# A transformer layer on one core: where the decay is multiplied in, how row maxima are taken and carried, and the order of the work

## The chip, the cores and the metric

The kernel runs on one core of one Trainium2 chip. The metric is the device time of one execution, in microseconds (us). A core has five engines that run their own instruction streams in order and wait for each other on semaphores: TensorE (PE, matrix products), VectorE (DVE), ScalarE (ACT), GpSimd (POOL) and SyncE (SP), which here only issues DMAs.

## The reference

The layer is a decayed quadratic attention plus a mixture of experts on the same normalised input. x is (4, 1024, 128). Cut to what the change touches:

```
qkvg = x @ w_attn                       # 16 query heads, 8 key/value heads, head size 64
q, k = rope(q), rope(k)
log_G = cumsum(log_sigmoid(6.906768 + gate), axis=time)
s = q . k / 8
logits = 2 * log|s| + log_G[t] - log_G[s]      # causal
a = exp(logits - max(logits))                  # so a is s*s*decay, over its row maximum
y = (a @ v) / (sum(a) + 1e-6)
y = (y - mean(y)) / sqrt(var(y) + 1e-9) * ln_w
out = x + y @ w_proj + experts(x)              # 7 routed experts, top 2, and one shared
```

The kernel never forms logits. It squares the scores, multiplies by the decay, and needs the row maximum of the weighted squares only for the small term 1e-6 and 1e-9 of the norm.

## The kernel before, in words

The work has a setup (input norm, routing, the shared expert, decay sums; about the first 150 us), a loop over 32 **pairs** and a tail. A pair p is one batch element and one key/value head with its two query heads (`hd` 0 and 1). Keys are shared by a **double pair**, so key rotation, value projection, the output projection `wp`, the norm (`ss`, `scales`, `roots`, `spread`, `norm`) come once for two pairs. "Even" and "odd" pair below mean p even and p odd.

Within a pair the 1024 queries are 4 spans of 256 (`m`, taken in the order 0, 2, 1, 3; `w` is the place in that order), and each span has one **diagonal step** (i = 0) and m **other steps** (i = 1 to m), each of two key blocks of 128. That makes 10 steps a pair: 4 diagonal, 6 other. A step's scores are 128 keys by 2 heads by 2 blocks by 256 queries, in a pair of PSUM banks; three such pairs of banks (`PAIRS`) are shared with all other products. TensorE takes steps in batches of 5 (`BATCH`): it computes 5 steps' scores, then the side jobs that are due (projections of q, k, v for later pairs, `wp`, `ss`, expert products), then the products with V for steps whose squares are ready. A job's bank is given by `bank_plan`, and TensorE waits until the bank's last content has been read.

An other step is read from PSUM by ScalarE, squared into a tile A (8 of them); its decay is split in a factor per query, which cancels in the norm, and a factor per key, `ES`. Before the change the key factor goes into V (GpSimd: `scale_values`, tiles VS) and, for the maximum, into VectorE's `scalar_tensor_tensor` with the per-partition operand `es`. A diagonal step has a true 2D decay D (ScalarE's exp, two instructions, then GpSimd's triangular `select`); VectorE multiplies PSUM by D (`diagonal`), ScalarE squares the tile in place.

The maxima run on VectorE in PSUM bank 5 (`PRUN`): per span one first maximum of a step with the diagonal tile, a half-width one, and one for each further block, then `fold`, a transposing reduction to 16 columns of `MR`. SyncE moves each fold's result by 4 small DMAs (`rows`) into `MF`. Once per double pair `scales` (16 small VectorE instructions in a row) makes the inverse norms; they go to HBM (`roots`), come back broadcast (`spread`), and GpSimd multiplies Y by them (`norm`).

The order on each engine is written by hand in tables (`PE_AT`, `ACT_AT`, `DVE_AT`, `POOL_AT`, `SP_AT`): a time in ticks, 20 for a pair, for each kind of work. The ticks only sort; nothing waits for a tick. Routed experts run in seven pairs (`EXPERT_PAIRS`), after all 64 `scatter` DMAs of GpSimd.

Of the kernel before, what the change touches and what calls it, by code (L numbers as in the profile page):

```python
# [19 lines left out]
GUARD = 1e-8  # L20
# [19 lines left out]
EXPERT_PAIRS, EARLY = (9, 12, 15, 18, 21, 24, 27), 6  # L40
# [10 lines left out]
             ("hl", 110.14, 0, 0, 1, 1), ("one", 132.74, 0, 0, 1, 1), ("forget", 117.51, 0.77, 0, 44, 1),  # L51
# [8 lines left out]
ACT_AT = [(12.8, "nt", 0), (27.18, "nt", 1), (-3.54, "decay", 0), (-3.53, "decay", 1), (5.4, "decay", 2),  # L60
          (10.31, "decay", 3), (36, "sq", 0), (29, "sq", 1), (8.58, "xe", 0), (21.82, "up", 0), (23.77, "up", 1), (25.18, "up", 2), (44.23, "up", 3),
          (61.99, "down", 0), (-22.23, "k", 0), (-21.67, "k", 1), (-10.3, "q", 0), (-10.17, "q", 1), (-9.65, "v", 0),
          (10.34, "v", 1), (5.99, "square", 0), (6.69, "square", 1), (13.39, "square", 2), (13.44, "square", 3),
          (13.8, "square", 4), (13.89, "square", 5), (7.75, "weigh", 0), (10.73, "weigh", 1), (12.4, "weigh", 2),
          (14.9, "weigh", 3)]
# [63 lines left out]
def wanted(kind, i, p):  # L129
# [3 lines left out]
    if kind in ("wp", "ss", "scales", "roots", "spread"):  # L133
        return p % 2 == 1
# [1446 lines left out]
```

## Time and profile before

| | |
|---|---|
| median of 3 runs | 1122.92 us (1121.73 to 1135.89) |
| the profiled execution's own time | 1129.5 us |
| its span, first to last instruction | 1127.4 us |
| mean granted TensorE clock | 0.933 of full |
| busy: PE, DVE, ACT, POOL | 943.9, 862.7, 613.5, 551.9 us |

Busy time is the time in which the engine had an instruction in work. The profiled execution took 6.6 us more than the median. An idle engine costs something only where another waits for it.

### The profile page before, as it was taken

To read this page: it belongs to the slowest core of one execution; us is meant where nothing else is said; L and a number is where in the kernel's file an instruction comes from. 1 tells how busy PE (TensorE), PEld (TensorE's weight loads), DVE (VectorE), ACT (ScalarE), POOL (GpSimd) and SP (SyncE) were. 2 spreads that over 40 slices of the span, in tenths; PEclk is the share of its full clock that TensorE was granted. 3 is DMA by queue.
4 is the path that set the end of the run, shared out by engine and by line. 5 is a ranking of instruction groups with operands and counts; after the bars stand their busy time and mean duration, and the time that the engine had idled before them with its cause. 6 is when DMAs were issued, how large, how long until landed. Compare 5 with 4: busy or idle time off the path is not lost.

```text
span 1127.4 us, 22306 instructions
## 1 busy us (share of the span) xinstructions
PE 943.9 (84%) x8487; PEld 672.6 (60%) x8487; DVE 862.7 (77%) x1555; ACT 613.5 (54%) x949; POOL 551.9 (49%) x561
## 2 busy tenths in 40 slices
PE   4999997979697969899988889896989898779861
PEld 3774665656475647576656566574657565557641
DVE  6679468887979785878786877878587978687882
ACT  2334265646555646567656657664656665665530
POOL 0311457767777644265536354635436553646421
PEclk9999998989999899899998999998899999899986
DMA  9201222242414242153325253424225342524253
GB/s 260 73 1 43 52 63 72 64 102 63 101 44 116 60 112 62 43 124 79 91 75 109 58 126 74 101 67 102 54 59 126 78 95 73 108 58 102 44 130 106
DMA packets 97659, 95.00 MB, mean 84 GB/s; under 512 B 33517, under 2 KB 82541, under 8 KB 97424
## 3 DMA queue, kind: packets, MB, share of 16 engines
q1 hardware_dynamic: 92480, 90.90, 33.0%
q0 software_dynamic: 5072, 2.67, 1.7%
q8 instruction: 67, 1.10, 0.4%
q14 instruction: 40, 0.33, 0.1%
HBM read 48.42 MB, written 13.46 MB: 55 GB/s over the span
## 4 chain that ended last, share of the span: by engine, by line
PE 41%; DVE 29%; SPq 8%; issue 7%; DMA 6%; POOL 5%; ACT 3%; POOLq 0%; DVEq 0%; ACTq 0%
PE PS L567 14%; PE PS L745 10%; PE PS L778 7%; DVE PS L1331 6%; DVE PS L1324 4%; DVE U L1331 4%; SPq L482 3%; SPq L453 2%; PE PS L610 2%; PE PS L620 2%; PE PS L613 2%; DVE MR L1344 2%; DMA SQ<-R_d 2%; SPq L499 2%; DMA U<-in_w 2%
## 5 line engine op out<-in xcount | busy, mean ns | idle before, releaser
L745 PE MATMUL PS<-Qt,Kt 64*128 64x256 f32 (+1 forms) x2560 | 304.5, 391 | 82.6 <-issue 17.5
L745 PEld LDWEIGHTS PS<-Qt,Kt 64*128 64x128 f32 x2560 | 252.5, 205 | 127.4 <-issue 39.9
L1464 POOL TENSOR_SCALAR_AFFINE_SELECT U<-U 128x256 f32<-128x256 f32 x128 | 54.9, 507 | 288.7 <-ACT U L849 288.4
L912 ACT ACTIVATE U<-PS 128x1024 f32<-128x1024 f32 x144 | 142.0, 1023 | 97.1 <-PE PS L745 89.0
L1442 POOL TENSOR_TENSOR U<-U,consts 128x512 f32<-128x512 f32 x96 | 130.4, 1358 | 73.9 <-DMA U<-U 73.5
L778 PE MATMUL PS<-U 128*64 128x256 f32 (+1 forms) x1344 | 141.3, 351 | 3.5 <-ACT U L908 3.5
L1294 DVE SCALAR_TENSOR_TENSOR U<-PS,U 128x768 f32<-128x768 f32 x96 | 88.6, 948 | 59.2 <-PE PS L745 45.8
L778 PEld LDWEIGHTS PS<-U 128*64 128x64 f32 x1344 | 93.4, 139 | 47.5 <-issue 13.2
L567 PE MATMUL PS<-XT,W 128*64 128x512 f32 x384 | 104.4, 651 | 11.8 <-DVE U L1294 11.5
L1331 DVE SCALAR_TENSOR_TENSOR PS<-U,ES,PS 128x512 f32<-128x512 f32 x144 | 108.4, 753 | 5.7
L908 ACT ACTIVATE U<-U 128x768 f32<-128x768 f32 x96 | 79.2, 842 | 58.0 <-DVE U L1294 56.9
L849 ACT ACTIVATE U<-U,negG 128x256 f32<-128x256 f32 (+1 forms) x256 | 97.8, 446 | 17.8 <-DMA U<-H_d 17.3
L1510 POOL TENSOR_TENSOR U<-U,SQ 128x1024 f32<-128x1024 f32 x32 | 77.1, 2410 | 39.0 <-DMA SQ<-R_d 38.9
L1344 DVE TRANSPOSE_TENSOR_REDUCE MR<-U 128x16 f32<-128x512 f32 x128 | 91.1, 711 | 4.4
L567 PE MATMUL PS<-U 128*64 128x128 f32 (+1 forms) x560 | 69.2, 390 | 23.2 <-DMA U<-in_w 16.3
L1445 POOL TENSOR_TENSOR Qt<-Qt,U 128x512 f32<-128x512 f32 x64 | 84.0, 1313 | 9.2
L1324 DVE SCALAR_TENSOR_TENSOR PS<-U,ES 128x512 f32<-128x512 f32 x64 | 75.0, 1172 | 16.6 <-ACT U L908 13.1
L859 ACT ACTIVATE U<-PS 128x512 f32<-128x512 f32 x64 | 37.9, 594 | 80.9 <-PE PS L567 80.8
L567 PE MATMUL PS<-Wp,U 128*64 128x128 f32 x1024 | 60.2, 277 | 25.7 <-POOL U L1510 25.7
L1474 POOL DMA_INDIRECT xe_d<-U,idx_s x64 | 67.1, 1048 | 24.3 <-issue 12.3
L567 PEld LDWEIGHTS PS<-Wp,U 128*64 128x64 f32 x1024 | 58.4, 140 | 33.6 <-POOL U L1510 26.2
L912 ACT ACTIVATE AX<-PS 128x1024 f32<-128x1024 f32 x48 | 48.0, 1024 | 49.3 <-PE PS L745 45.0
(179 smaller groups left out, 1536.1 us busy)
## 6 DMA issues: line engine op xcount, KB each, us to landing
U<-U SPq DMA_DIRECT2D x192, 128.0 KB
U<-H_d SPq DMA_DIRECT2D x32, 512.0 KB
SQ<-R_d SPq DMA_DIRECT2D x64, 256.0 KB, 5.7
Kt<-Kt SPq DMA_DIRECT2D x32, 256.0 KB
U<-MR SPq DMA_DIRECT2D x512, 2.0 KB
U<-in_w SPq DMA_DIRECT2D x21, 256.0 KB
acc<-in_x SPq DMA_DIRECT2D x4, 512.0 KB, 5.3
ye_d<-SQ SPq DMA_DIRECT2D x4, 512.0 KB, 8.2
```

The source lines that it names most:

```text
L567: mm = te.matmul(to[lo:lo + 64], weights[:, lo:lo + 64], moving, start=start, stop=stop)
L745: mm = te.matmul(bank[:, 256 * n:256 * n + 256 - lo], Kt[u % 2][(ki + hd) % 2][rows, 128 * j:128 * j + 128], Qt[p % 2][m // 2][rows, 256 * ...
L778: mm = te.matmul(P[4][64 * hd:64 * hd + 64, c + lo:c + 256], vt, A[s % NA][:, o:o + 256 - lo], start=begins and n == 0, stop=ends and n == 1)
L849: ex = s.activation(D[un % 3][:, lo:hi], HR[:, 256 * m + 128 * k2:256 * m + 256], ACT.Exp, scale=0.5, bias=negG[:, n:n + 1])
L908: s.activation(a_, a_, ACT.Square).then_inc(a_sd, 1)
L912: s.activation(A[n % NA], PS[:, first:first + 1024], ACT.Square, scale=0.125, bias=GUARD).then_inc(a_so, 1)
L1294: v.scalar_tensor_tensor(A[s % NA].rearrange("p (a t) -> p a t", a=2)[:, :, 0:384], PS[:, first:first + 1024].rearrange("p (a t) -> p a t" ...
L1324: v.scalar_tensor_tensor(PRUN, a_[:, :, 0], es, diag[:, :, 0], ALU.mult, ALU.max).then_inc(v_mx, 1)
L1331: v.scalar_tensor_tensor(run if i == m and n == 1 else PRUN, a_[:, :, n], es, PRUN, ALU.mult, ALU.max).then_inc(v_mx, 1)
L1344: v.tensor_reduce(MR[:, c:c + 16], RUN.rearrange("p (b r) -> p b r", r=32), AX, ALU.max, apply_transpose=True).then_inc(v_red, 1)
L1442: g.tensor_tensor(sw, sw, sinT[:, cols], ALU.mult).then_inc(made, 1)
L1445: g.tensor_tensor(to, to, sw, ALU.add).then_inc(added, 1)
```

## The change

1. **Key factor into the square.** ScalarE squares an other step in two instructions, one for each key block, with a per-partition scale (`ES`, now the square root of the key factor over 8) and bias (`ESG`). V is used as it is, and the tiles VS and `scale_values` are gone.
2. **Plain maxima.** The running maxima on VectorE are `tensor_tensor` max, without the factor.
3. **One diagonal step in four weighted by GpSimd** (`HEAVY`, the step of span m = 3): ScalarE squares it straight from PSUM, with D made as the full decay (`negH`), and GpSimd multiplies the square by D (`weigh`). VectorE has no part in it.
4. **Maxima through HBM.** Instead of 4 DMAs for each fold, one store of 128 columns and 4 loads a double pair (`tops`, `rows`).
5. **`scales` in 3 parts**, placed apart from each other.
6. **A new order** in all tables; the experts run two pairs later (11 to 29 in place of 9 to 27), and the scatter DMAs are spaced 3.6 ticks apart, not 2.8.

```diff
-EXPERT_PAIRS, EARLY = (9, 12, 15, 18, 21, 24, 27), 6
+HEAVY = [(3,)] * 32
+EXPERT_PAIRS, EARLY = (11, 14, 17, 20, 23, 26, 29), 6
...
-SCATTER_AT = [14 * c / 5 for c in range(64 - EARLY)]
+SCATTER_AT = [18 * c / 5 for c in range(64 - EARLY)]
...
+SP_AT = [(19.81, 'tops', 0), (27.85, 'rows', 0), (-25.05, 'swapk', 0), (-24.57, 'swapq', 0), (-16.51, 'keys', 0), (-18.91, 'row', 0), (-12.19, 'weights', 0), (-8.02, 'weights', 1), (35.08, 'roots', 0), (36.5, 'spread', 0)]
...
-            return (a_sd, 4 * p + w + 1) if i == 0 else (a_so, 6 * p + sum(n > 0 for _, n in STEPS[:k + 1]))
+            if i:
+                return a_so, 6 * p + sum(n > 0 for _, n in STEPS[:k + 1])
+            return (g_dw if w in HEAVY[p] else a_sd), weighed(p, w)
+
+        def weighed(p, w):
+
+            heavy = sum(map(len, HEAVY[:p])) + sum(n in HEAVY[p] for n in range(w))
+            return (heavy if w in HEAVY[p] else 4 * p + w - heavy) + 1
...
-            def rows(p, w):
-
-                m, u, c = ORDER[w], p // 2, 16 * (4 * (p % 4) + w)
-                sp.wait_ge(v_red, 4 * p + w + 1)
+            def store_tops(u):
+
+                sp.wait_ge(v_red, 8 * u + 8)
+                if u > 1:
+                    sp.wait_ge(s_g[u % 2], 64 * (u // 2))
+                sy.dma_start(M_d[128 * (u % 2):128 * (u % 2) + 128], MR[:, 128 * (u % 2):128 * (u % 2) + 128]).then_inc(s_md, 16)
+
+            def rows(u):
+
+                sp.wait_ge(s_md, 16 * (u + 1))
                 if u > 1:
                     sp.wait_ge(v_m, u - 1)
-                for j in range(4):
-                    o = 128 * (u % 2) + 64 * (p % 2) + 16 * j
-                    sy.dma_start(MF[32 * m:32 * m + 32, o:o + 16],
-                                 MR[32 * j:32 * j + 32, c:c + 16]).then_inc(s_g[u % 2], 16)
+                for w, m in enumerate(ORDER):
+                    sy.dma_start(MF[32 * m:32 * m + 32, 128 * (u % 2):128 * (u % 2) + 128].rearrange("r (p j c) -> r p j c", p=2, j=4),
+                                 M_v[u % 2, w]).then_inc(s_g[u % 2], 16)
...
-                    pe.wait_ge(g_vs, 3 * p + w)
+                    pe.wait_ge(a_v, 2 * u + (2 * m - 1) // 4 + 1)
...
-                        if i == 0:
-                            vt = Vt[u % 2].rearrange("p (k n d) -> p k n d", k=NB, d=64)[:, j, hu]
-                        else:
-                            vt = VS[m][:, 64 * j:64 * j + 64]
+                        vt = Vt[u % 2].rearrange("p (k n d) -> p k n d", k=NB, d=64)[:, j, hu]
...
-                    ac.wait_ge(v_t, 4 * p + w + 1)
-                    s.activation(a_, a_, ACT.Square).then_inc(a_sd, 1)
+                    if w in HEAVY[p]:
+                        free(n)
+                        first = 512 * BANK["score", n]
+                        ac.wait_ge(p_s, 2 * n + 2)
+                        s.activation(a_, PS[:, first:first + 1024].rearrange("p (a t) -> p a t", a=2)[:, :, 0:384],
+                                     ACT.Square, scale=0.125, bias=GUARD).then_inc(a_sh, 1)
+                    else:
+                        ac.wait_ge(v_t, weighed(p, w))
+                        s.activation(a_, a_, ACT.Square).then_inc(a_sd, 1)
                 else:
                     first = 512 * BANK["score", n]
                     ac.wait_ge(p_s, 2 * n + 2)
-                    s.activation(A[n % NA], PS[:, first:first + 1024], ACT.Square, scale=0.125,
-                                 bias=GUARD).then_inc(a_so, 1)
+                    ac.wait_ge(v_es, 1)
+                    for t, j in enumerate(blocks):
+                        c = ES_AT[m] + 16 * m * (p // 8) + KVH * j + p % 8
+                        sq = s.activation(A[n % NA].rearrange("p (a n t) -> p n a t", a=2, n=2)[:, t],
+                                          PS[:, first:first + 1024].rearrange("p (a n t) -> p n a t", a=2, n=2)[:, t],
+                                          ACT.Square, scale=ES[:, c:c + 1], bias=ESG[:, c:c + 1])
+                    sq.then_inc(a_so, 1)
...
+                ve.wait_ge(a_es, 1)
+                v.tensor_scalar(ESG[:, :], ES[:, :], GUARD, None, ALU.mult).then_inc(v_es, 1)
+                chain(v.tensor_scalar(ES[:, :], ES[:, :], 0.125, None, ALU.mult))
...
-                for n, j in enumerate(blocks):
-                    c = ES_AT[m] + 16 * m * (p // 8) + KVH * j + p % 8
-                    es = ES[:, c:c + 1]
-                    if i == 1 and n == 0:
-                        ve.wait_ge(v_add, 8)
-                        ve.wait_ge(v_mx, done)
-                        v.scalar_tensor_tensor(PRUN, a_[:, :, 0], es, diag[:, :, 0], ALU.mult, ALU.max).then_inc(v_mx, 1)
-                        ve.wait_ge(v_mx, done + 1)
-                        v.tensor_tensor(PRUN[:, :, 128:256], PRUN[:, :, 128:256], diag[:, :, 1, 0:128],
-                                        ALU.max).then_inc(v_mx, 1)
-                        done += 2
-                    else:
-                        ve.wait_ge(v_mx, done)
-                        v.scalar_tensor_tensor(run if i == m and n == 1 else PRUN, a_[:, :, n], es, PRUN, ALU.mult,
-                                               ALU.max).then_inc(v_mx, 1)
-                        done += 1
+                if i == 1:
+                    ve.wait_ge(v_add, 8)
+                    ve.wait_ge(v_mx, done)
+                    v.tensor_tensor(PRUN, a_[:, :, 0], diag[:, :, 0], ALU.max).then_inc(v_mx, 1)
+                    ve.wait_ge(v_mx, done + 1)
+                    v.tensor_tensor(PRUN[:, :, 128:256], PRUN[:, :, 128:256], diag[:, :, 1, 0:128], ALU.max).then_inc(v_mx, 1)
+                    done += 2
+                for n in range(1 if i == 1 else 0, 2):
+                    ve.wait_ge(v_mx, done)
+                    v.tensor_tensor(run if i == m and n == 1 else PRUN, a_[:, :, n], PRUN, ALU.max).then_inc(v_mx, 1)
+                    done += 1
...
-                    ve.wait_ge(s_g[u % 2], 512 * (u // 2))
+                    ve.wait_ge(s_md, 16 * (u - 1))
...
-            def scales(u):
...
+            def scales(u, part):
...
+                if part == 0:
+                    ve.wait_ge(s_g[u % 2], 64 * (u // 2 + 1))
...
+                elif part == 1:
+                    ve.wait_ge(v_f, at + 4)
+                    v.tensor_tensor(dens_v, ys_v[:, 4:8], ZT_v[:, 4:8], ALU.mult).then_inc(v_f, 1)
...
+                else:
+                    y, y_v, t, t_v = ys[:, 0:32], ys_v[:, 0:4], ts[:, 0:32], ts_v[:, 0:4]
+                    for n in range(2):
...
-            def scale_values(p, w):
-                u, hu, m = p // 2, p % 2, ORDER[w]
...
+            def weigh(p, w):
+
+                n = 10 * p + DIAGONAL[w]
+                a_ = A[n % NA].rearrange("p (a t) -> p a t", a=2)[:, :, 0:384]
+                po.wait_ge(a_sh, weighed(p, w))
+                po.wait_ge(g_sel, 4 * p + w + 1)
+                g.tensor_tensor(a_, a_, bc(D[(4 * p + w) % 3], 1, 2), ALU.mult).then_inc(g_dw, 1)
...
+                elif kind == "heavy":
+                    if i in HEAVY[p]:
+                        weigh(p, i)
```

On VectorE, between an even pair and the odd pair behind it (pairs 10 and 11). Before, the rows of `fold` (MR), the last key rotation (Kt), then `scales` as one piece from the reduction to the last transposition, then the odd pair's diagonal steps (PS,U with 384 columns):

```order
L1331 SCALAR_TENSOR_TENSOR U<-U,ES,PS 128x512
L1344 TENSOR_REDUCE MR<-U 128x16
L1282 TENSOR_TENSOR Kt<-PS,consts 128x512
L1350 TENSOR_REDUCE SM<-U 128x32
L1356 STREAM_TRANSPOSE U<-PS 128x256
L1359 TENSOR_SCALAR SM<-U 128x64
L1361 TENSOR_TENSOR SM<-SM 128x64
...
L1385 SCALAR_TENSOR_TENSOR U<-SM 128x4x8
L1388 STREAM_TRANSPOSE U<-U 128x256
L1294 SCALAR_TENSOR_TENSOR U<-PS,U 128x2x384 x2
```

With the change, the same place, the first part of `scales` left out here (it stands ahead of the maxima of span m = 3, after the fold of m = 1):

```order
L1349 TENSOR_TENSOR U<-U,PS 128x512
L1361 TENSOR_REDUCE MR<-U 128x16
L1316 SCALAR_TENSOR_TENSOR U<-PS,U 128x2x384 x2
L1398 TENSOR_TENSOR SM<-SM 128x32
L1400 SCALAR_TENSOR_TENSOR SM<-SM 128x32
L1403 SCALAR_TENSOR_TENSOR SM<-SM 128x32
L1398 TENSOR_TENSOR SM<-SM 128x32
L1400 SCALAR_TENSOR_TENSOR SM<-SM 128x32
L1405 SCALAR_TENSOR_TENSOR U<-SM 128x4x8
L1408 STREAM_TRANSPOSE U<-U 128x256
L1316 SCALAR_TENSOR_TENSOR AX<-PS,U 128x2x384
```

Two diagonal steps have moved ahead of the last part of `scales`, and one stands behind it; the transposition that reads the bank of `ss` has moved ahead of the last span's maxima.

On GpSimd, in an odd pair and at its end (pair 11). Before, with the second key half, then the first half of the next q, the norm of the first pair of the double pair, the second half of q, the norm of the other:

```order
L1445 TENSOR_TENSOR Kt<-Kt,U 128x512
L1442 TENSOR_TENSOR U<-U,consts 128x512
L1445 TENSOR_TENSOR Qt<-Qt,U 128x512
L1510 TENSOR_TENSOR U<-U,SQ 128x1024
L1442 TENSOR_TENSOR U<-U,consts 128x512
L1445 TENSOR_TENSOR Qt<-Qt,U 128x512
L1510 TENSOR_TENSOR U<-U,SQ 128x1024
```

With the change (a select stands between the second key half and these rows):

```order
L1462 TENSOR_TENSOR U<-U,consts 128x512
L1465 TENSOR_TENSOR Qt<-Qt,U 128x512
L1523 TENSOR_TENSOR U<-U,SQ 128x1024
L1473 TENSOR_TENSOR U<-U 128x2x384
L1462 TENSOR_TENSOR U<-U,consts 128x512
L1465 TENSOR_TENSOR Qt<-Qt,U 128x512
L1479 AFFINE_SELECT U<-U 128x2x128 x3
L1523 TENSOR_TENSOR U<-U,SQ 128x1024
```

The weighing (L1473) has come between the norm and the second half of the next q.

On SyncE, one double pair in the middle of the loop. Before (MR are the folds' DMAs, U<-U 32x1024 the swaps of the rotation, SQ<-R_d the spread, Kt<-Kt the key copies):

```order
L491 DMA R_d<-U 128x256
L453 DMA U<-U 32x1024 x4
L499 DMA SQ<-R_d 64x4x256 x4
L482 DMA U<-MR 32x16 x4
L428 DMA U<-H_d 128x1024
L482 DMA U<-MR 32x16 x4
L471 DMA Kt<-Kt 64x1024
L472 DMA Kt<-Kt 64x1024
```

With the change:

```order
L491 DMA R_d<-U 128x256
L448 DMA U<-U 32x1024 x4
L499 DMA SQ<-R_d 64x4x256 x4
L423 DMA U<-H_d 128x1024
L466 DMA Kt<-Kt 64x1024
L467 DMA Kt<-Kt 64x1024
```

The 8 small DMAs ahead of the key copies are gone; the spread still stands behind the four swaps.

## Rows read from the trace of the kernel before

**Rows 1.** Busy in loop and tail: PE, PEld, DVE, ACT, POOL; clock, DMA share, GB/s.
```profile
150.00:1080.00 930.00, 797.68 (x7577) 571.92 (x7575) 741.85 (x1155) 554.90 (x862) 508.60 (x509) 0.93 0.35 83
1080.00:1127.00 47.00, 17.14 (x216) 14.05 (x212) 23.86 (x45) 6.60 (x8) 9.37 (x4) 0.75 0.47 120
```

**Rows 2.** Waits of TensorE inside the loop: us in total, times, longest.
```profile
PE PS L745 <- issue: 17.5, 7, 3.0
PE PS L745 <- DMA Kt<-Kt: 16.8, 8, 3.8
PE PS L745 <- DVE U L1356: 16.8, 8, 3.7
PE PS L745 <- POOL Qt L1445: 16.6, 5, 5.5
PE PS L567 <- DMA U<-in_w: 16.3, 4, 6.0
PE PS L562 <- DVE U L1294: 13.1, 6, 3.6
PE PS L567 <- DVE U L1294: 11.5, 5, 3.1
PE PS L745 <- DVE U L1265: 10.1, 5, 4.1
```

**Rows 3.** Timeline of TensorE over one odd pair: start, length, work, idle before it.
```profile
705.27 4.09 PE L745 MATMUL PS<-Qt,Kt 64*128 64x256 f32 x40 [2.03 <-issue]
...
732.22 4.67 PE L745 MATMUL PS<-Qt,Kt 64*128 64x256 f32 x40 [2.02 <-DMA Kt<-Kt]
```

**Rows 4.** One window of three microseconds behind a gap; columns as in Rows 1.
```profile
309.00:312.00 3.00, 2.46 (x12) 2.03 (x14) 2.15 (x3) 0.87 (x3) 2.85 (x3) 0.50 0.02 5
```

**Rows 5.** Groups by line: count, busy us, mean ns; VectorE's.
```profile
L1331 DVE SCALAR_TENSOR_TENSOR PS<-U,ES,PS 128x512 f32<-128x512 f32 x144 | 108.4, 753 | 5.7
...
L1294 DVE SCALAR_TENSOR_TENSOR U<-PS,U 128x768 f32<-128x768 f32 x96 | 88.6, 948 | 59.2 <-PE PS L745 45.8 <-POOL U L1464 13.0 <-issue 0.3
...
L1324 DVE SCALAR_TENSOR_TENSOR PS<-U,ES 128x512 f32<-128x512 f32 x64 | 75.0, 1172 | 16.6 <-ACT U L908 13.1 <-DVE MR L1344 0.5
...
L1232 DVE TENSOR_TENSOR U<-U,PS 128x512 f32<-128x512 f32 x32 | 21.8, 682 | 23.5 <-PE PS L613 12.3 <-ACT U L811 11.1
...
L1361 DVE TENSOR_TENSOR SM<-SM 128x64 f32<-128x64 f32 x16 | 5.7, 354 | 0.5
```

**Rows 6.** Groups by line, ScalarE's and GpSimd's.
```profile
L912 ACT ACTIVATE U<-PS 128x1024 f32<-128x1024 f32 x144 | 142.0, 1023 | 97.1 <-PE PS L745 89.0 <-issue 6.2 <-DVE PS L1326 1.7
...
L1442 POOL TENSOR_TENSOR U<-U,consts 128x512 f32<-128x512 f32 x96 | 130.4, 1358 | 73.9 <-DMA U<-U 73.5 <-issue 0.2
...
L1510 POOL TENSOR_TENSOR U<-U,SQ 128x1024 f32<-128x1024 f32 x32 | 77.1, 2410 | 39.0 <-DMA SQ<-R_d 38.9
...
L1456 POOL TENSOR_TENSOR U<-U,ES 128x256 f32<-128x256 f32 x64 | 39.3, 615 | 50.1 <-PE PS L778 42.2 <-DVE U L1232 7.6
...
L811 ACT ACTIVATE U<-PS 128x512 f32<-128x512 f32 x32 | 18.9, 596 | 27.7 <-PE PS L610 26.0 <-DVE U L1232 1.4
...
L805 ACT ACTIVATE U<-PS,GB 128x512 f32<-128x512 f32 x8 | 6.2, 777 | 12.2 <-PE PS L594 12.2
```

**Rows 7.** Timeline of ScalarE in the second batch of a pair.
```profile
691.76 2.85 ACT L912 ACTIVATE U<-PS 128x1024 f32<-128x1024 f32 x3 [0.49 <-PE PS L745]
```

**Rows 8.** Timeline of SyncE's DMA queue in the odd pair.
```profile
715.82 2.43 SPq L453 DMA_DIRECT2D U<-U  x4
718.35 2.64 SPq L499 DMA_DIRECT2D SQ<-R_d  x4
...
727.68 0.60 SPq L471 DMA_DIRECT2D Kt<-Kt  x1
```

**Rows 9.** The chain that ended last, in the tail: start, us, what.
```profile
1104.28 1.71 DMA R_d<-U
...
1106.70 6.12 DMA SQ<-R_d
```

More of the change, by code:

```diff
@@ L60 @@
[L60 to L65, printed above, removed]
@@ L76 @@
+SCATTER_AT = [18 * c / 5 for c in range(64 - EARLY)]
 GATES_AT = [SCATTER_AT[32 - EARLY] - 1]
 SP_FIRST = [("row", 0), ("swapk", 0), ("swapq", 0), ("keys", 0)]
-SP_AT = [(-1.59, "rows", 0), (8.46, "rows", 1), (9.68, "rows", 2), (11.17, "rows", 3), (-29.72, "swapk", 0),
-         (-25.73, "swapq", 0), (-11.27, "keys", 0), (-14.53, "row", 0), (-10.6, "weights", 0), (4.79, "weights", 1), (32, "roots", 0), (34.5, "spread", 0)]
+SP_AT = [(19.81, 'tops', 0), (27.85, 'rows', 0), (-25.05, 'swapk', 0), (-24.57, 'swapq', 0), (-16.51, 'keys', 0), (-18.91, 'row', 0), (-12.19, 'weights', 0), (-8.02, 'weights', 1), (35.08, 'roots', 0), (36.5, 'spread', 0)]
@@ L132, in wanted @@
         return p % 2 == 0 and p > 0
-    if kind in ("wp", "ss", "scales", "roots", "spread"):
+    if kind in ("wp", "ss", "scales", "roots", "spread", "tops", "rows"):
         return p % 2 == 1
@@ L157, in job_of @@
 def job_of(kind, p, i):
-    if kind in ("k", "v", "swapk", "keys", "wp", "ss", "scales", "roots", "spread"):
+    if kind in ("k", "v", "swapk", "keys", "wp", "ss", "scales", "roots", "spread", "tops", "rows"):
         return kind, p // 2, i
@@ L275, in block_program @@
         ZT, RT, RR, MF = (take(256) for _ in range(4))
-        VS0 = take(384)
+        take = carve(20224)
         HR = take(1024)
@@ L510, in place @@
                     load_decay_row(u)
+                elif kind == "tops":
+                    store_tops(u)
                 elif kind == "rows":
-                    rows(u, i)
+                    rows(u)
                 elif kind == "roots":
@@ L827, in setup @@
                     ac.wait_ge(v_esd, 1)
-                    s.activation(ES[:, :], ES[:, :], ACT.Exp).then_inc(a_es, 1)
+                    s.activation(ES[:, :], ES[:, :], ACT.Exp, scale=0.5).then_inc(a_es, 1)
                 elif kind == "e1":
@@ L849, in decays @@
                     ex = s.activation(D[un % 3][:, lo:hi], HR[:, 256 * m + 128 * k2:256 * m + 256], ACT.Exp,
-                                      scale=0.5, bias=negG[:, n:n + 1])
+                                      scale=1.0 if w in HEAVY[p] else 0.5,
+                                      bias=(negH if w in HEAVY[p] else negG)[:, n:n + 1])
                 ex.then_inc(a_d, 1)
@@ L1287, in diagonal @@
                 un = 4 * p + w
+                if w in HEAVY[p]:
+                    return
                 ve.wait_ge(g_sel, un + 1)
@@ L1400, in _ @@
                 elif kind == "scales":
-                    scales(p // 2)
+                    scales(p // 2, i)
                 elif kind == "gates":
```

149 lines of the change are left out of this document (64 added, 85 removed).

## The prediction

> **What bounds the kernel now.** I read the busy times by stretch first. In the loop (150 to 1080 us) TensorE is busy 797.7 of 930 us, VectorE 741.9, ScalarE 554.9, GpSimd 508.6 [rows 1]. The change adds and removes no product of TensorE, so the loop can give back two things: TensorE's idle time, 930 - 797.7 = 132.3 us, and what its slow clock costs. The granted clock is 0.93 over the loop, so about 0.07 x 797.7 = 56 us of the busy time are there only because it was not full. It falls behind gaps: after the 5.3 us gap that ends at 309.5 us the next window stands at 0.50, the lower level, though TensorE works in most of it [rows 4]. Together 188 us, 58.1 us a double pair being spent (930 / 16) where 46.4 would do.
>
> Then the list of TensorE's waits [rows 2]: no one cause holds it. 16.8 us for the transposition of `ss`'s bank (L1356), 13.1 + 11.5 for the diagonal steps (L1294), 16.8 for the key copies, 16.6 for the rotated q, 16.3 for expert weights, 10.1 for the expert products on VectorE (L1265), 17.5 with no releaser seen. The timeline shows that they sit in and around odd pairs: one starts at 705.3 and the next pair at 732.2 us, 26.9 us [rows 3], though an odd pair has no `wp`, `ss` or k products and only some 19 us of TensorE's work (two score bursts of 4.1 us or more, q, v and two runs of products with V, by my count).
>
> **The change, part by part.** *VectorE.* 32 of its 128 diagonal multiplications go: 32 x 0.95 = 30 us [rows 5]. The 288 maxima of L1331 (four groups of this form, 144 of them in the row) become a plain maximum: 0.753 against 0.682 us for a plain two-input operation of 512 columns with one input in PSUM (L1232), so 288 x 0.07 = 20 us. The 96 first maxima (L1324) have both inputs in SBUF and show 1.17 us, but only because some are stretched. The plain L1361 is stretched too: 64 columns take 0.35 us on average, over half as long as 512 columns in PSUM form. I take it that the stretch stays, and credit 96 x 0.07 = 7. Sum 57 us of 742.
> The Trainium skill (VectorE: DVE Perf Modes and GPSIMD Engine Reference, in the table of the engine's properties) has the two engines share an SBUF interface and contend when VectorE's instruction has two SBUF inputs. By that rule the stretch stays whatever the operation, and the relief is 57 us; were it the mark of the form with a factor, it would be 96 x (1.12 - 0.68) = 42 in place of 7, that is 92 us.
>
> *ScalarE.* Two instructions of 512 columns, scale and bias each a per-partition operand, in place of one of 1024. The near row is L805, 0.777 us with two such operands, against 0.596 for L811 with none [rows 6]. Back to back they overlap: three of 1.023 last 2.85, so 0.1 each [rows 7]. A step is then 2 x 0.68 = 1.36 in place of 0.95, and 192 steps cost +79 us of busy time. What of it is on the path: in a pair's second batch all five steps are now read by ScalarE (4 x 1.36 + 0.8 = 6.2 us, the 0.8 for 768 columns between the 0.6 and 1.02 of 512 and 1024, against a score burst of 4.1 to 4.7). With three pairs of banks the fifth score waits for the second read only, which ends in time; the side jobs behind wait for the third and fourth. I put 0.4 us a pair, +13 us. The bounds are 0 (other work in between) and the whole 79. The extra table loads and the decays are unchanged.
>
> *GpSimd.* The VS products go, 39.3 us for one group and, by length, some 27 for the 32 longer ones of 384 columns; 32 weighings of 768 columns come, between 1.36 (512) and 2.41 us (1024), so 1.9 each, 60 us [rows 6]. Busy time is level. But the weighing stands ahead of the second half of the next q, and behind a `norm` that waits for the spread. In an odd pair that starts at 0: scores to 4.4, q products to 6.6, ScalarE's copy and four swap DMAs (2.4 us of SyncE) to 9.5, spread issue 2.6 [rows 8] and its landing 6.1 from the first issue [rows 9] to about 16, norm 2.4 to 18.5, weighing 1.9, q 2.7: 23. The next pair's first score needs that half. So an odd pair can't fall to 19 but to some 23 or 24, from 27. The added 1.9 us counts where this chain is last: 16 odd pairs, in the end a fifth of it, +6 us. Bounds 0 and 30.
>
> *Maxima through HBM.* 512 small DMAs, 0.63 us of SyncE each, become 80. Nothing is late for the store and the loads: a fold's result is wanted a pair later, and the store is like the 1.71 us one of the roots [rows 9]. Key copies were issued at 727.7, and between the spread's last issue at 721.0 and them SyncE had eight of the small ones and one row load [rows 8]; their 16.8 us of waits should mostly go: -12.
>
> *Norm in three parts.* The transposition that frees `ss`'s bank moves ahead of the last span's maxima: its 16.8 go. Two of three diagonal steps move ahead of the last part, about 2.2 us of VectorE in place of 6 or more ahead of all three: of 24.6, -15. With VectorE 57 us lighter, -5 of the 10.1 behind expert products. The second weight load is issued far earlier: -8 of 16.3. Of q's 16.6 and the unexplained 17.5, -10, q now being projected before `wp`. Sum of gains in idle time: 12 + 16.8 + 15 + 5 + 8 + 10 = 67.
>
> *Clock.* Half the gaps gone does not mean half of the slow stretches: the one behind the odd pair stays. A third of 56: -18.
>
> *Setup and tail.* Two small operations on ES come in the setup, beside others: 0. In the tail the 8 adds of the experts' output (5.5 us of VectorE) move behind the norm, where it waits for the spread, but the last maxima now make a store and a load, some 5 us, before `scales`; and a 512 KB load is issued ahead of the spread. +2, bounds -4 and +6.
>
> Sum: -67 - 18 + 13 + 6 + 2 = -64. From the profiled 1129.5 that is 1065.5; the median lies 6.6 us below that execution, so **1059 us**. Check by the other way: a double pair of 58.1 becomes about 54 (odd 27 to 24, even 1 less by the clock and expert waits), 16 x 4.1 = 66.
>
> **The rivals.** *A, full relief.* The waits are one knot: when the pieces come early, all but the odd pair's own chain goes. 100 of the 132 us and 40 of the 56, against +21: -119, or 1004 us; say 1000 to 1030. For it: VectorE would be at 685 of some 810 us, not full. Against it: the spread's chain above, counted at 23 us.
> *B, the wait changes its place.* The chain spread, norm, weighing, q sets odd pairs at 25 or 26 us, ScalarE's later reads fill what the maxima saved, and only some 2 us a double pair go, with little clock: -32 - 5 + 15, or 1101 us (1090 to 1115). For it: the norm and q are in a row on one engine, and GpSimd's scatters now last to the tenth pair.
> *C, slower: ScalarE becomes the bound.* Its loop work is 555 + 79 = 634 us, 40 us a double pair and more where experts add table loads, and its order mixes copies that others wait for with squares. If each square's 0.41 us lands on the path, +79 in place of 13, and the relief on VectorE is worth only half (-33, no clock): 1129.5 + 79 + 6 + 2 - 33 = 1183, 1177 as a median. It decides from the point where ScalarE's busy share in the loop nears 85%; I compute 634 / 866 = 73%.
> *D, the stretch was the form's* (the first reading of L1324): 35 us less on VectorE, of which a quarter counts, 9 us: 1050, inside my forecast.
>
> **How the numbers follow.** A measurement of this kernel tells about 2% from no change. The forecast with D (1030 to 1090) has 0.47, A 0.23, B 0.21, C 0.09. The likeliest time is 1059. Range 1000 to 1112: it takes the forecast, A but for its far end, and most of B. Faster by over 2% is below 1100.5: the forecast, A, and some 0.08 of B, 0.78. Slower by 2% is C, 0.09 with its milder half counted as same: 0.08. Same 0.14.
>
> **What would show it.** In the profile after: VectorE's busy total near 805 us, the former L1331 at 0.68, the first maxima with a maximum of well over 1 us; ScalarE's near 690, the halves at 0.78; SyncE's DMA count down by 432. TensorE's wait for the transposition gone, that for key copies below 5 us, and odd pairs of 23 to 25 us; the clock at 0.95. The prediction is wrong if TensorE's waits name ScalarE's squares (C), or if those for the rotated q grow over 40 us (B); or if the waits without a releaser, which I credit blindly, stay.

## The result and the profile after

The changed kernel takes 1091.1 us in the median of 4 runs (1084.85 to 1095.47), the kernel before 1127.53 us in 4 runs: a ratio of 0.967 with an interval of 0.958 to 0.976. It is faster by 36 us; 64 were forecast. The profiled execution was the slowest of the four, 1095.47 us; its span is 1093.7, its mean granted clock 0.935, where the other three have 0.944 to 0.949.

The busy totals, and the loop (columns as in Rows 1; it now ends about 1046):

```profile
PE 950.6 (87%) x8487; PEld 666.8 (61%) x8487; DVE 812.5 (74%) x1526; ACT 685.9 (63%) x1141; POOL 554.7 (51%) x497
```
```profile
150.00:1046.00 896.00, 807.16 (x7611) 568.31 (x7611) 695.22 (x1131) 629.79 (x1054) 506.83 (x444) 0.94 0.39 87
```

The loop went from 930 to 896 us, 56.0 us a double pair in place of 58.1 [rows 1]. TensorE's idle time in it fell from 132.3 to 88.8 us, but its busy time rose from 797.7 to 807.2, where the forecast had it fall by 18.

TensorE's waits in the loop, after:

```profile
PE PS L748 <- DMA Kt<-Kt: 40.5, 13, 3.9
PE PS L778 <- POOL U L1473: 19.9, 7, 5.7
PE PS L748 <- ACT U L924: 7.3, 30, 0.4
PE PS L748 <- ACT U L886: 4.7, 4, 1.4
...
PE PS L748 <- ACT AX L924: 3.8, 13, 0.4
PE PS L748 <- POOL Qt L1465: 2.9, 2, 1.6
PE PS L570 <- DVE U L1316: 2.0, 3, 0.7
```

Beside [rows 2], the list is a new one. The transposition's 16.8 us and the expert weights' 16.3 are gone, the diagonal steps' 24.6 are 2.0, the rotated q's 16.6 are 2.9, and nothing is left without a releaser. But the key copies hold TensorE for 40.5 us, 13 times in 16 double pairs, where they held it for 16.8; the new weighing holds it for 19.9; and ScalarE's longer reads take 7.3 + 3.8.

SyncE's queue in an odd pair, TensorE's timeline at its two ends, and the stretches behind the spread and behind the gap (columns as in Rows 1: clock, DMA share and GB/s are the last three):

```profile
686.40 3.74 SPq L448 DMA_DIRECT2D U<-U  x4
690.24 2.65 SPq L499 DMA_DIRECT2D SQ<-R_d  x4
692.93 1.09 SPq L423 DMA_DIRECT2D U<-H_d  x1
694.06 0.99 SPq L466 DMA_DIRECT2D Kt<-Kt  x1
695.09 2.31 SPq L467 DMA_DIRECT2D Kt<-Kt  x1
```
```profile
678.62 3.63 PE L748 MATMUL PS<-Qt,Kt 64*128 64x256 f32 x32
...
707.08 6.42 PE L748 MATMUL PS<-Qt,Kt 64*128 64x256 f32 x40 [3.94 <-DMA Kt<-Kt]
```
```profile
694.00:698.00 4.00, 3.96 (x58) 3.44 (x58) 3.05 (x5) 4.00 (x7) 1.35 (x2) 1.00 1.03 211
698.00:702.00 4.00, 4.00 (x46) 2.83 (x44) 0.31 (x1) 1.24 (x2) 4.00 (x3) 1.00 1.08 214
...
706.50:708.00 1.50, 0.92 (x4) 0.90 (x6) 1.43 (x3) 0.65 (x3) 1.50 (x2) 0.50 0.59 170
```

The reader is to see three things. The copies are issued at once behind the spread and the row load, as foreseen. Their second one lands 11.9 us after its issue at 695.1, in a stretch where the DMA engines are busy all the time, at some 210 GB/s. And this odd pair lasts 28.5 us (678.6 to 707.1); the forecast was 24, before were 26.9 [rows 3]. The burst behind the gap then takes 6.42 us instead of 4.1: the granted clock stands at 0.50, its lower level, in the last row.

GpSimd and VectorE at the same place:

```profile
697.45 2.36 POOL L1523 TENSOR_TENSOR U<-U,SQ 128x1024 f32<-128x1024 f32 x1 [2.65 <-DMA SQ<-R_d]
699.77 1.82 POOL L1473 TENSOR_TENSOR U<-U 128x768 f32<-128x768 f32 x1
701.53 1.28 POOL L1462 TENSOR_TENSOR U<-U,consts 128x512 f32<-128x512 f32 x1
702.96 1.52 POOL L1465 TENSOR_TENSOR Qt<-Qt,U 128x512 f32<-128x512 f32 x1
```
```profile
701.69 1.68 DVE L1343 TENSOR_TENSOR PS<-U 128x512 f32<-128x512 f32 x1 [4.41 <-POOL U L1473]
```

Here is the forecast's chain of spread, norm, weighing and q. It ends at 704.5, 25.9 us into the pair, and is not even last: the keys are, at 706.95. VectorE's first maximum waits 4.41 us for the weighing.

Groups that answer to [rows 5] and [rows 6], and TensorE's largest one, which had 304.5 us before:

```profile
L748 PE MATMUL PS<-Qt,Kt 64*128 64x256 f32 (+1 forms) x2560 | 325.6, 402 | 67.6 <-DMA Kt<-Kt 40.5 <-ACT U L924 10.1 <-ACT U L886 4.7
...
L924 ACT ACTIVATE U<-PS,ESG,ES 128x512 f32<-128x512 f32 x288 | 203.1, 793 | 38.6 <-PE PS L748 38.6
...
L1343 DVE TENSOR_TENSOR PS<-U 128x512 f32<-128x512 f32 x64 | 69.7, 1089 | 72.5 <-POOL U L1473 67.6 <-ACT U L924 2.9
L1349 DVE TENSOR_TENSOR PS<-U,PS 128x512 f32<-128x512 f32 x144 | 99.7, 692 | 5.5
```

### The profile page after: what moved, and what is told of

It reads as the page before. It is cut to its first block, busy times and chain, and to the rows that moved or that the text cites. A ratio compares the mean times of both kernels' runs of the same rounds, so it can differ in the third digit from the quotient of the medians.

```text
span 1093.7 us, 21986 instructions
## 1 busy us (share of the span) xinstructions
PE 950.6 (87%) x8487; PEld 666.8 (61%) x8487; DVE 812.5 (74%) x1526; ACT 685.9 (63%) x1141; POOL 554.7 (51%) x497
## 4 chain that ended last, share of the span: by engine, by line
PE 43%; DMA 18%; DVE 15%; SPq 9%; ACT 7%; issue 5%; POOL 3%; POOLq 0%; DVEq 0%; ACTq 0%
PE PS L570 12%; PE PS L748 12%; DMA Kt<-Kt 7%; PE PS L778 7%; DMA U<-H_d 6%; SPq L499 3%; SPq L448 3%; ACT U L924 3%; PE PS L613 2%; PE PS L616 2%; PE PS L623 2%; DMA SQ<-R_d 2%; DVE U L1316 2%; ACT U L850 1%; DVE PS L1349 1%
## 5 line engine op out<-in xcount | busy, mean ns | idle before, releaser
L748 PE MATMUL PS<-Qt,Kt 64*128 64x256 f32 (+1 forms) x2560 | 325.6, 402 | 67.6 <-DMA Kt<-Kt 40.5
L924 ACT ACTIVATE U<-PS,ESG,ES 128x512 f32<-128x512 f32 x288 | 203.1, 793 | 38.6 <-PE PS L748 38.6
L778 PE MATMUL PS<-U 128*64 128x256 f32 (+1 forms) x1920 | 204.8, 361 | 20.8 <-POOL U L1473 19.9
L778 PEld LDWEIGHTS PS<-U 128*64 128x64 f32 x1920 | 133.3, 138 | 93.8 <-POOL U L1473 24.1
L1479 POOL TENSOR_SCALAR_AFFINE_SELECT U<-U 128x256 f32<-128x256 f32 x128 | 54.8, 431 | 182.8 <-ACT U L850 181.9
L1343 DVE TENSOR_TENSOR PS<-U 128x512 f32<-128x512 f32 x64 | 69.7, 1089 | 72.5 <-POOL U L1473 67.6
L1349 DVE TENSOR_TENSOR PS<-U,PS 128x512 f32<-128x512 f32 x144 | 99.7, 692 | 5.5
L850 ACT ACTIVATE U<-U,negG 128x256 f32<-128x256 f32 x192 | 75.2, 468 | 44.2 <-DMA U<-H_d 44.1
L1316 DVE SCALAR_TENSOR_TENSOR U<-PS,U 128x768 f32<-128x768 f32 x72 | 67.0, 946 | 36.1 <-PE PS L748 33.8
L924 ACT ACTIVATE AX<-PS,ESG,ES 128x512 f32<-128x512 f32 x96 | 68.0, 792 | 19.8 <-PE PS L748 19.8
L778 PE MATMUL PS<-AX,U 128*64 128x256 f32 (+1 forms) x640 | 71.9, 358 | 0.0
```

The lines of the kernel that those rows point to most:

```text
L748: mm = te.matmul(bank[:, 256 * n:256 * n + 256 - lo], Kt[u % 2][(ki + hd) % 2][rows, 128 * j:128 * j + 128], Qt[p % 2][m // 2][rows, 256 * ...
L778: mm = te.matmul(P[4][64 * hd:64 * hd + 64, c + lo:c + 256], vt, A[s % NA][:, o:o + 256 - lo], start=begins and n == 0, stop=ends and n == 1)
L850: ex = s.activation(D[un % 3][:, lo:hi], HR[:, 256 * m + 128 * k2:256 * m + 256], ACT.Exp, scale=1.0 if w in HEAVY[p] else 0.5, bias=(negH ...
L924: sq = s.activation(A[n % NA].rearrange("p (a n t) -> p n a t", a=2, n=2)[:, t], PS[:, first:first + 1024].rearrange("p (a n t) -> p n a t ...
L1316: v.scalar_tensor_tensor(A[s % NA].rearrange("p (a t) -> p a t", a=2)[:, :, 0:384], PS[:, first:first + 1024].rearrange("p (a t) -> p a t" ...
L1343: v.tensor_tensor(PRUN, a_[:, :, 0], diag[:, :, 0], ALU.max).then_inc(v_mx, 1)
```

## The experiments

Each number is a ratio to the kernel before, run beside it on the same chip; the change itself stands at 0.967. So 0.01 is 11 us. The change was not run again beside the experiments, and its own interval is 0.018 wide, so a distance from it is known to some 12 us only, and that between two experiments to some 8. No experiment leaves anything out of the computation unless it is said.

**Keys ahead of the spread.** The change, with the key copies issued as soon as GpSimd has rotated them (in the trace of the change it had at 684.3 us, and they were issued at 694.1), ahead of swaps, spread and row load:

```diff
-SP_AT: (-16.51, 'keys', 0)
+SP_AT: (-25.0, 'keys', 0)
```

> The changed kernel with the key copies placed ahead of the roots' store on SyncE, one number in the order table. Theory 1 (queue): TensorE's 40.5 us of waits for the key copies come from their place behind the spread (1 MB) and the decay row (512 KB); the trace shows them issued at 694.1 and landing 11.9 us after the second issue, though GpSimd had finished the keys at 684.3. They then land in about 4 us, the wait falls below 8 us, and the rotated q or ScalarE is late next, about 2.4 us earlier: 1091 - 40 = 1050 (1040 to 1065). Theory 2 (the chain of norm, weighing and q is as long): the wait only changes its name, 1085 or more.

Measured: 1073.97 us, 0.948 (0.942 to 0.953), some 21 us under the change. TensorE's wait for the copies is gone. Its waits, and a row of the chain that ended last in the same odd pair (676.7 to 702.5, 25.9 us):

```profile
PE PS L778 <- POOL U L1473: 33.0, 10, 7.6
PE PS L748 <- POOL Qt L1465: 22.5, 14, 2.0
```
```profile
691.39 10.33 DMA U<-H_d
```

The place in the queue was the cause. The 512 KB row load, now last behind the spread, is the one that takes 10.3 us to land; ScalarE waits for such loads 13.7 us in all, at most 2.8 at a time. The list shows who was next all along: GpSimd's weighing and q, 55.5 us together.

**The maxima through HBM, alone.** The kernel before, with one store and four loads a double pair in place of 32 small DMAs, at the ticks 11.17 and 27.85:

```diff
-                for j in range(4):
-                    sy.dma_start(MF[32 * m:32 * m + 32, o:o + 16], MR[32 * j:32 * j + 32, c:c + 16])
+                for w, m in enumerate(ORDER):
+                    sy.dma_start(MF[32 * m:32 * m + 32, 128 * (u % 2):128 * (u % 2) + 128].rearrange(...), M_v[u % 2, w])
```

> The kernel before with one thing of the change: the maxima through HBM, one store and four loads a double pair in place of 32 small DMAs. SyncE loses some 270 us of issuing. Theory 1 (my prediction's reasoning): the key copies are issued up to 6 us earlier, their 16.8 us of waits go: 12 to 25 us faster than before. Theory 2 (the DMA queue holds the keys back, behind the spread and the decay row, whoever issues): within 8 us of before, the wait for the key copies 16 us or more.

Measured: 1149.0 us, 1.013 (1.008 to 1.017): slower by little, where the forecast had a gain. TensorE's waits (its lines lie ten further on here), and the key copies in the chain that ended last:

```profile
PE PS L755 <- DMA Kt<-Kt: 38.0, 9, 6.2
PE PS L577 <- DMA U<-in_w: 33.2, 4, 9.0
```
```profile
722.44 10.01 DMA Kt<-Kt
```

This is the point where the forecast broke. The same copy in the kernel before was issued at 728.32 and took 3.76 us: it landed at 732.1. Issued 5.9 us earlier it takes 10.0 and lands at 732.45. Taking the small DMAs out only moved the time from SyncE's issuing into the transfer, behind the spread's 1 MB and the row's 512 KB, and left the expert weights worse placed.

**The small DMAs back in the change.** The change, with maxima carried as before, at the ticks -1.59, 8.46, 9.68 and 11.17.

> The changed kernel with the maxima carried as before, 4 small DMAs for each fold at their old places in SyncE's order. On the kernel before the carriage through HBM alone cost 1.25% (+14 us). Theory 1 (it is a loss in the change too, because it lets the decay row and the key copies crowd behind the spread; the tail has its store and loads exposed besides): 8 to 20 us faster than the changed kernel, ratio to before 0.950 to 0.960. Theory 2 (in the new order the small DMAs would hold the swaps and the keys back): slower than the changed kernel, 0.975 or more.

Measured: 1100.16 us, 0.971 (0.965 to 0.977), no difference from the change that these runs can tell. The key copies' wait falls to 5.1 us, but:

```profile
PE PS L770 <- POOL U L1465: 53.9, 12, 7.9
PE PS L740 <- POOL Qt L1457: 21.3, 13, 2.0
```

75 us of waits for the weighing and q (other line numbers, the same operations). So the HBM path shows neither gain nor loss in the change, within some 12 us; the stall goes to whichever of the two is later. The second copy is issued at 709.08 us here, 4.3 us behind the spread's last issue and not 2.2 as in the change, and takes 7.75 us: it lands 12.0 us behind that issue, as it does with the HBM path in the kernel before (12.0), and near the 11.1 of the kernel before itself. Whenever it is issued, it lands 11 to 14 us behind the spread.

**The keys earlier, in the kernel before.** They come right behind the spread, ahead of one fold's DMAs and the row load; a place ahead of the spread, as in the change, was not tried here.

```diff
-SP_AT: (-11.27, "keys", 0)
+SP_AT: (-22.5, "keys", 0)
```

> The kernel before with only the key copies moved on SyncE, to right behind the spread, ahead of one fold's DMAs and of the decay row (512 KB). The keys are ready at 721.8 us in the trace of before and issued at 727.7. Theory 1 (their place in the DMA queue sets the wait, also without the change): TensorE's 16.8 us of waits for them fall below 6, 8 to 15 us faster. Theory 2 (the odd pair is held by VectorE and the rotated q as well): within 6 us of before.

Measured: 1160.22 us, 1.025 (1.021 to 1.029), slower, which neither theory had. Its TensorE waits, and SyncE's queue around the copies:

```profile
PE PS L567 <- DMA U<-in_w: 36.6, 6, 9.6
PE PS L745 <- POOL Qt L1445: 23.2, 9, 6.5
```
```profile
729.25 0.51 SPq L471 DMA_DIRECT2D Kt<-Kt  x1
...
730.45 3.90 SPq L482 DMA_DIRECT2D U<-MR  x4
734.39 0.58 SPq L428 DMA_DIRECT2D U<-H_d  x1
```

There GpSimd rotates the keys late, so SyncE stands at the copies (17.2 us in 13 waits) with the row load and the expert weights behind it: ScalarE's wait for the row goes from 17.3 to 49.9 us, TensorE's for the weights from 16.3 to 36.6. TensorE's wait for the copies is indeed gone (0.7 us). With the keys early in the change, SyncE stands at the copies even longer, 120.3 us in 15 waits, but nothing behind them is due then, and that kernel gains 21 us; this one loses 28. That it loses them by this standing is read from the waits; no run separates it.

**No weighing on GpSimd.** The change, with all diagonal steps on VectorE; and this together with the early keys.

```diff
-HEAVY = [(3,)] * 32
+HEAVY = [()] * 32
```

> The changed kernel with no diagonal step weighed by GpSimd: VectorE multiplies all four again. Theory 1: the weighing's 19.9 us of waits on TensorE and 67.6 us on VectorE vanish, but 30 us of VectorE come back, and the key copies still end the odd pair: within 10 us of 1091. Theory 2 (the weighing pays by VectorE's 30 us): 1105 or more. Theory 3 (the weighing is itself the loss, it stands ahead of q): 1075 or less.

> The changed kernel with the key copies ahead of the roots' store and no weighing by GpSimd. Each alone gave 21 and 13 us over the changed kernel. With the keys early TensorE waited 33.0 us for the weighing and 22.5 for the rotated q, both at the end of the chain spread, norm, weighing, q. Theory 1: that chain gets 1.8 us shorter each odd pair and the value products no longer wait: a ratio to before of 0.925 to 0.935 (1045 to 1058). Theory 2 (VectorE's 30 us more are on the path by now): 0.945 or more.

Measured: 1081.2 us, 0.956 (0.951 to 0.961), without the weighing: the third part of the change costs some 12 us, just about clear of the noise (the intervals overlap a little). With early keys 1065.4 us, 0.940 (0.936 to 0.944), 9 less than with early keys alone. Without the weighing VectorE's total is 816.4 us, against 812.5 with it, though it does 32 more products of 0.95 us. The reason shows in two of its rows, with the weighing and, in the second fence, without; the last two fences have GpSimd and VectorE at one of the long ones, with the weighing:

```profile
L1381 DVE SCALAR_TENSOR_TENSOR SM<-SM,U 128x64 f32<-128x64 f32 x16 | 17.1, 1067 | 0.5
```
```profile
L1343 DVE TENSOR_TENSOR PS<-U 128x512 f32<-128x512 f32 x64 | 61.4, 959 | 3.2
...
L1381 DVE SCALAR_TENSOR_TENSOR SM<-SM,U 128x64 f32<-128x64 f32 x16 | 4.3, 272 | 0.6
```
```profile
670.96 1.34 POOL L1465 TENSOR_TENSOR Qt<-Qt,U 128x512 f32<-128x512 f32 x1
```
```profile
671.20 1.23 DVE L1381 SCALAR_TENSOR_TENSOR SM<-SM,U 128x64 f32<-128x64 f32 x1
```

A 64-column operation takes 1.07 us on average in the kernel with the weighing and 0.27 in the one without; L1343 goes from 1.09 to 0.96. Beside the long ones stands not the weighing itself but the second half of q's rotation, in 13 of 16 double pairs; the weighing, 1.82 us ahead of it on GpSimd, is what moves it there, for without the weighing it stands beside none of the 16. Of the 30 us that the weighing takes off VectorE, some 27 come back.

**One square a step.** The change, with each other step read by one instruction of 1024 columns. This leaves out the key factor of the decay (of the squares and the maxima).

```diff
-                    for t, j in enumerate(blocks):
-                        sq = s.activation(..., ACT.Square, scale=ES[:, c:c + 1], bias=ESG[:, c:c + 1])
+                    sq = s.activation(A[n % NA], PS[:, first:first + 1024], ACT.Square, scale=0.125, bias=GUARD)
```

> The changed kernel with one square of 1024 columns and constant factors in place of two with per-partition operands; it leaves out the key factor of the decay, so its output is another. ScalarE loses some 75 us of busy time. Theory 1 (my sum): 13 us on the path, 1078, seen as score bursts of 4.4 in place of 4.8 us. Theory 2 (ScalarE's reads are on the path in most steps): 1050 or less.

Measured: 1072.36 us, 0.946 (0.941 to 0.952): the two reads cost some 23 us by the ratios, where 13 were put; at 12 us of noise the 13 are not excluded. Second batches of two pairs, in the change and in this kernel:

```profile
690.67 2.65 PE L748 MATMUL PS<-Qt,Kt 64*128 64x256 f32 x24
693.51 2.00 PE L748 MATMUL PS<-Qt,Kt 64*128 64x256 f32 x16 [0.19 <-ACT U L924]
```
```profile
677.92 4.41 PE L748 MATMUL PS<-Qt,Kt 64*128 64x256 f32 x40
```

2.65 + 0.19 + 2.00 = 4.84 us against 4.41. The burst stops for a read ahead of its fourth score, which the forecast had excluded ("the fifth score waits for the second read only, which ends in time").

**`scales` in one piece again.** The change, with its three parts in a row.

```diff
-DVE_AT: (25.81, 'scales', 0), (31.28, 'scales', 1), (36.95, 'scales', 2)
+DVE_AT: (33.4, 'scales', 0), (33.41, 'scales', 1), (33.42, 'scales', 2)
```

> The changed kernel with the three parts of the norm's scales in one row again, just ahead of the odd pair's first diagonal step, as before the change. Theory 1: the waits for the transposition and the diagonal steps come back in part (16.8 and 24.6 us before), 1091 + 25 to 40 = 1115 to 1130. Theory 2 (with the key copies last, the odd pair hides them): within 8 us of 1091.

Measured: 1153.54 us, 1.018 (1.012 to 1.024): it loses 58 us, more than the change gained. VectorE and GpSimd there, then TensorE and its largest wait:

```profile
714.32 1.19 DVE L1379 TENSOR_TENSOR SM<-SM 128x64 f32<-128x64 f32 x1
715.55 0.27 DVE L1381 SCALAR_TENSOR_TENSOR SM<-SM,U 128x64 f32<-128x64 f32 x1
715.85 1.19 DVE L1383 SCALAR_TENSOR_TENSOR SM<-SM 128x64 f32<-128x64 f32 x1
```
```profile
714.09 1.34 POOL L1462 TENSOR_TENSOR U<-U,consts 128x512 f32<-128x512 f32 x1
715.58 1.38 POOL L1465 TENSOR_TENSOR Kt<-Kt,U 128x512 f32<-128x512 f32 x1
```
```profile
722.66 3.68 PE L570 MATMUL PS<-XT,W 128*64 128x512 f32 x8 [3.57 <-DVE U L1316]
```
```profile
PE PS L570 <- DVE U L1316: 42.1, 10, 5.7
```

The piece falls beside the key rotation. Four small operations of some 0.2 us take 1.14 to 1.19 us each, the block lasts 8.4 us (713.4 to 721.8), and the diagonal steps behind it hold a bank that TensorE wants: 42.1 us of waits, and 16.0 more of the same kind in another group of its products, where the change has 2.0. How much of that is the stretch and how much the place of the piece is not separated.

**`scales` in three parts, alone.** The kernel before, with the same three parts at 25.42, 28.1 and 39.3.

> The kernel before with one thing of the change: scales in three parts, the first after the fold of span m = 1, the second behind the first maxima of span m = 3, the third ahead of the third diagonal step of the odd pair. One piece in the changed kernel cost +58 us over it (1153.5 against some 1094 on that chip). Theory 1 (the parts are the main gain of the change by themselves): 30 to 60 us faster than before, TensorE's waits for the transposition gone. Theory 2 (they pay only in the new order, where GpSimd rotates keys at that time and stretches each small operation to 1.2 us): within 15 us of before.

Measured: 1120.55 us, 0.988 (0.985 to 0.992). The waits for the transposition and for the diagonal steps go (0 and 0.8 us), which were 41.4; a new one stands in their place, for the key product's read on VectorE:

```profile
PE PS L745 <- DVE Kt L1282: 51.3, 22, 4.3
```

**Plain maxima, alone.** The kernel before, with `tensor_tensor` maxima; the factor of the key is left out of the maxima.

> The kernel before with plain maxima in place of those with a factor; it leaves the key factor out of the maxima, so the small term of the norm is another. VectorE loses 20 us for the maxima with one input in PSUM (0.75 to 0.69 us each) and, as the stretch of the first maxima stayed in the changed kernel, few more. Theory 1: 8 to 20 us faster. Theory 2 (VectorE's length does not matter outside the scales block): within 6 us of before.

Measured: 1127.88 us, 0.996 (0.992 to 1.000). L1324 goes from 1.172 to 1.088 us and L1331 from 0.753 to 0.692: the stretch stays with the plain form.

**Both GpSimd pieces placed.** Early keys, and the norm of the first pair behind the second half of q: `norm` from 68.29 to 69.9, ScalarE's `sq` behind it from 36.73 to 47.9. The second kernel drops the weighing as well.

> The changed kernel, weighing kept, with the key copies ahead of the roots' store and the norm of the even pair moved behind the second half of the next q on GpSimd (and ScalarE's square of that Y later by the same need). Theory 1 (the norm, which waits for the spread, holds q and the weighing back): both waits, 33.0 and 22.5 us, mostly go, ratio 0.920 to 0.935. Theory 2 (the norm's delay then holds back the output projection in the even pair): 0.945 or more, with TensorE waiting for the norm.

> The changed kernel with all three edits that paid: the key copies ahead of the roots' store, the even pair's norm behind the second half of the next q, and no weighing by GpSimd. With the weighing 12.8 us of TensorE's waits were still for it. Theory 1: these go, ratio 0.925 to 0.933. Theory 2 (VectorE's 30 us more are now on the path, ScalarE's waits of 38 us stay): 0.935 to 0.942, no better than each of the pairs.

Measured: 1064.19 us, 0.937 (0.934 to 0.941), the lowest ratio here, 3% under the change; without the weighing 1063.34 us, 0.939 (0.933 to 0.945), the same. In the first, TensorE's timeline in an odd pair:

```profile
662.02 3.63 PE L748 MATMUL PS<-Qt,Kt 64*128 64x256 f32 x32
...
686.46 2.00 PE L748 MATMUL PS<-Qt,Kt 64*128 64x256 f32 x16
```

24.4 us, the 24 of the forecast. Once the weighing and q no longer stand behind the norm, which waits for the spread, the weighing costs nothing that these runs show (they tell 8 us): its 12 us were its place in that row, not its work. It still stands ahead of q's second half (678.4 and 680.7 us on GpSimd), and TensorE still waits 12.8 us for it; without it, TensorE waits longer for ScalarE's squares, 26.8 us in place of 13.6.

## Why the prediction was right in direction and too large

**What held.** The transposition's 16.8 us went, the diagonal steps lost 22.6 of 24.6 where 15 were credited, expert weights and expert products 25.9 of 26.4 (13 credited), q and the unexplained 31.2 of 34.1 (10 credited): 96.5 us against 54.8. One more wait without a releaser, of 6.9 us, went too. VectorE came to 812.5 us (805 forecast), ScalarE to 685.9 (690), GpSimd stayed level. For the first two the three parts of the norm are shown to be the cause: alone, in the kernel before, they take away both, though they are worth 13 us only, since a next wait moves in. For the others it is the order as a whole, of which no part was tried singly but the keys and the norm.

Rival D is refuted: the plain first maxima still average 1.09 us, in the change and alone in the kernel before, and the plain 64-column operation, with `scales` in one piece, takes 1.19 beside GpSimd's rotation. The Trainium skill's rule on the shared SBUF interface (GPSIMD Engine Reference, Specifications) agrees with that. (The forecast worked D out with 1.12 us where the row has 1.17, which is 5 us of VectorE's busy time and changes nothing.) The Trainium skill's price for a per-partition operand (ScalarE: Activation LUTs, What ACT_TABLE_LOAD costs; some 93 ns each) agrees with the trace: 0.793 us with two of them, 0.596 with none [rows 6].

**The step that failed** is "Maxima through HBM": "their 16.8 us of waits should mostly go: -12". They rose by 23.7, 36 us off. The prediction took the time ahead of the copies for SyncE's issuing time. Of it 6.7 us were, but [rows 8] show issues, not transfers: ahead of the copies stand 1 MB of spread and 0.5 of the row, and with their own 0.5 MB that is 2 MB, by an estimate some 10 us at the measured 210 GB/s. The maxima through HBM alone left the landing where it was for an earlier issue; the place ahead of the spread is the cure, worth some 21 us.

**The second one** is GpSimd's term, "in the end a fifth of it, +6": the new wait of TensorE for the weighing is 19.9 us in the trace, and removing the weighing gives some 12, inside the bounds of 0 and 30. The chain was put down rightly; left out was that the products with V of an odd pair and VectorE's maxima wait for the weighing itself (4.41 us above), not only q behind it.

**ScalarE's reads**, +13, measured some 23 with 12 of noise: by the ratio a term set too low, and the trace shows what was left out, score bursts that stop inside (11.1 us of waits).

**The clock**, -18, hardly came in the profiled execution: 0.933 to 0.935 over the span, 0.94 in the loop, and TensorE's busy time rose by 9.5 us in place of falling. The scores alone went from 304.5 to 325.6 us for the same 2560 products. That group has 310.2 us with the early keys and 307.9 with one square a step: the gap at the keys, with the slow burst behind it (6.42 us), and the stops inside bursts each account for much of it, and the two overlap. Elsewhere the clock followed the gaps as assumed: 0.953 with early keys, 0.961 without the weighing, 0.968 with both steps; but the kernel with the lowest ratio has only 0.952. And the change's profiled execution is its slowest: the other three, at 0.944 to 0.949, took 1084.85 to 1092.77 us. So some of the missing clock belongs to that one execution, and how much of the 18 us came in the median is open.

**Setup and tail**: the end behind the last `ss` took 35.5 us and takes 39.2, +3.7 where +2 was put. The store and the loads of the maxima are not the reason: the roots' store is issued 12.4 us behind `ss` before and 11.6 now. The spread is:

```profile
1069.83 10.49 DMA SQ<-R_d
```

Its last DMA took 6.12 us [rows 9], with the loads of the experts' output all issued well ahead of it; now one of these, of 512 KB, is issued right ahead of the spread and three right behind.

By the terms, TensorE's idle time in the loop was to fall by 67 and rise by 19, net 48, and fell by 43.5. That looks right and is not: the 96.5 and 6.9 us above stand against 23.7 for the keys, 19.9 for the weighing, 11.1 for the squares' reads and 4.7 for an expert copy of ScalarE's. Gains set too low and one sign wrong covered each other; most of the miss of 30 us in the profiled executions is TensorE's busy time, 9.5 + 18. Of the rivals, B had the right pattern (the wait changes its place), and 1091.1 lies at the edge of its 1090 to 1115, just outside the 1030 to 1090 of the forecast itself; but the waits it named came to 2.9 us for q, since the keys were later still. A is not borne out: with the waits for the keys and for the weighing gone too, the kernel still takes 1063 us, not 1004. C's mechanism is there at about a third of its price (some 23 of 79 us), at a busy share of 629.8 / 896 = 70%.

The effects don't add. The three parts are worth 13 us alone and 58 when undone in the change; keys moved ahead -21 us in the change, +28 before (at another place of the queue); the weighing 12, 9 and nothing as the other two waits go.

What stays open: what the 24.4 us of waits without a releaser in the kernel before were, and whether the change without its new order would gain at all; neither was tried.

## What to carry to other kernels

Ask of a late transfer how many bytes were queued ahead of it, not how many issues: an earlier issue behind the same bytes lands at the same time, while a place ahead of them takes the wait away, 40.5 us here, of which the kernel kept 21. Moved ahead of its data, though, it holds the queue for everything behind it, which is free only while nothing there is due. And work handed to GpSimd costs by its place in GpSimd's row and by what it stretches on VectorE; its own busy time says little.

## What the runs showed of the hardware

- A VectorE operation of 32 or 64 columns with its inputs in SBUF takes 0.2 to 0.3 us alone and 1.14 to 1.19 beside a GpSimd `tensor_tensor` of 1.3 us, `scalar_tensor_tensor` and plain alike: the starts differ, but each ends within 0.15 us of the GpSimd instruction beside it (715.51 and 715.43, 717.04 and 716.96). An operation of 512 columns goes from 0.67 to 1.68 us in the case shown, so a chain of small ones loses far more in proportion.
- A 256 KB copy inside SBUF with 1.5 MB issued ahead of it landed 3.8, 7.8, 10.0 and 11.9 us after its issue when it was issued 7.3, 4.3, 1.9 and 2.2 us behind the last of the first 1 MB, at a DMA share of 0.95 to 1.08 in the stretches where the queue was full. SyncE's issue itself grew from 0.60 us in the first case to 2.31 in the last.
- With its queue that full, a 512 KB load took 10.3 us, against a median of 5.3 in that kernel.
